# A two-layer transformer in fixed slots on one core: an even slot's gated products before its biases, layer norms on another engine, experts spread over every third slot

## The reference

```python
xn = _layernorm(x)
x = x + L0_attn(xn) + L0_ffn(xn)
xn = _layernorm(x)
x = x + L1_attn(xn) + L1_ffn(xn)
```

## Time and profile before

| | |
|---|---|
| runs | 2309.81, 2303.06, 2306.30 us; median 2306.3 us |
| profiled execution | 2310.34 us, its span 2308.5 us |
| PE busy | 2078.7 us, 90% |
| DVE busy | 1635.0 us, 71% |
| ACT busy | 1400.3 us, 61% |
| POOL busy | 1147.4 us, 50% |
| mean granted clock of PE | 0.971 |

### The profile page before, as it was taken

The page is one execution under the profiler, slowest core; times in us unless marked ns, Lnnn a source line. Parts: engine busy times, 40 slices in busy tenths (PEclk is TensorE's granted clock), DMA queues, the critical chain, the costliest instruction groups (busy, mean ns, idle before and its releaser), DMA issues.

```text
span 2308.5 us, 52509 instructions
## 1 busy us (share of the span) xinstructions
PE 2078.7 (90%) x18761; PEld 1355.0 (59%) x18761; DVE 1635.0 (71%) x5384; ACT 1400.3 (61%) x3797; POOL 1147.4 (50%) x1800
## 2 busy tenths in 40 slices
PE   3888989989899998989989899998989999898988
PEld 1455655656566574655656566574655656566565
DVE  7557767677777767767677776767767677766756
ACT  1667566665756657566665756657566575756642
POOL 5675463745536454463645636454463745535220
PEclk7779999999999999999999999999999999999999
DMA  4000000000000000000000000000000000000000
GB/s 119 6 6 2 1 15 1 15 2 11 6 2 15 1 15 2 1 15 2 15 2 7 10 2 15 2 15 2 1 15 2 15 2 11 1 2 11 2 10 6
DMA packets 33542, 22.03 MB, mean 10 GB/s; under 512 B 2443, under 2 KB 32771, under 8 KB 33283
## 3 DMA queue, kind: packets, MB, share of 16 engines
q1 hardware_dynamic: 33283, 18.68, 2.8%
HBM read 14.48 MB, written 4.19 MB: 8 GB/s over the span
## 4 chain that ended last, share of the span: by engine, by line
PE 60%; DVE 16%; ACT 13%; issue 8%; POOL 4%; DVEq 0%; ACTq 0%; POOLq 0%
PE ps L1097 9%; PE ps L1168 9%; PE ps L1178 7%; PE ps L1237 7%; PE ps L1111 6%; ACT ring L921 4%; PE ps L1087 3%; PE ps L1066 3%; DVE ring L538 3%; ACT pb L930 3%; PE ps L1075 2%; PE ps L1222 2%; PE ps L1144 2%; PE ps L1195 2%; PE ps L1207 2%
## 5 line engine op out<-in xcount | busy, mean ns | idle before, releaser
L814 POOL TENSOR_SCALAR ring<-ring,row_rcp,tau_row 128x128 f32<-128x128 f32 (+3 forms) x1024 | 626.1, 618 | 824.4 <-DVE row_rcp L545 824.2
L921 ACT ACTIVATE ring<-ring,neg_max 128x128 f32<-128x128 f32 (+3 forms) x1024 | 572.2, 560 | 625.6 <-DVE neg_max L538 622.3
L1097 PE MATMUL ps<-identf,ring 128*128 128x128 f32 x2560 | 384.9, 288 | 17.9 <-ACT qkT L912 11.3
L930 ACT ACTIVATE pb<-ps 128x512 f32<-128x512 f32 x640 | 349.1, 585 | 23.9 <-PE ps L1097 16.8
L538 DVE CUSTOM_DVE_ANT_1 ring<-ps,bias_t 128x384 f32<-128x384 f32 (+1 forms) x496 | 287.2, 615 | 82.3 <-PE ps L1087 78.3
L1097 PEld LDWEIGHTS ps<-identf,ring 128*128 128x128 f32 x2560 | 280.1, 144 | 103.8 <-issue 62.6
L1168 PE MATMUL ps<-xn1T,eg_t 128*128 128x512 f32 (+1 forms) x480 | 265.1, 635 | 37.2 <-DVE h L592 36.9
L1237 PEld LDWEIGHTS ps<-ed_t,h 128*128 128x128 f32 (+1 forms) x1920 | 250.7, 191 | 74.7 <-issue 73.1
L1237 PE MATMUL ps<-ed_t,h 128*128 128x128 f32 (+1 forms) x1920 | 272.3, 278 | 0.0
L1178 PE MATMUL ps<-xn1T,eu_t 128*128 128x512 f32 (+1 forms) x480 | 259.3, 622 | 0.4 <-DVE h L599 0.4
L944 ACT ACTIVATE tanh_t<-ps 128x512 f32<-128x512 f32 (+2 forms) x304 | 171.9, 565 | 123.0 <-PE ps L1168 118.3
(11 more groups left out here) (161 smaller groups left out, 3208.2 us busy)
## 6 DMA issues: line engine op xcount, KB each, us to landing
x_t<-x SPq DMA_DIRECT2D x16, 256.0 KB, 2.8
x<-x SPq DMA_DIRECT2D x16, 256.0 KB, 2.8
out<-x SPq DMA_DIRECT2D x16, 256.0 KB, 2.3
bias_t<-bias SPq DMA_DIRECT2D x1, 1536.0 KB, 7.7
eg_t<-eg SPq DMA_DIRECT2D x1, 860.0 KB
eu_t<-eu SPq DMA_DIRECT2D x1, 860.0 KB
ed_t<-ed SPq DMA_DIRECT2D x2, 320.0 KB
ring<-inv_row SPq DMA_DIRECT2D x1, 256.0 KB, 2.7
```

The costliest lines, as they stand in the source:

```text
L814: pool.tensor_scalar(e, e, row_rcp[:, m % 2, r:r + 1], tau_row[:, i, HG * g + r:HG * g + r + 1], ALU.mult, ALU.add).then_inc(p_ok.sem, 1)
L921: act.activation(e, e, ACT.Exp, bias=neg_max[:, n % 2, r:r + 1], scale=-1.0, accum_out=row_sum[:, n % 2, r:r + 1]).then_inc(exp_ok.sem, 1)
L930: act.activation(pb[:, c % NPB, :], bank(turn_bank(q)), ACT.Relu).then_inc(t_taken[q % 2].sem, 1)
L1097: last = pe.transpose(o[:, r * P:(r + 1) * P], ring_of(i, r)[:, k * P:(k + 1) * P], idf)
```

## The change

1. On DVE the gated products (`products`) of an even slot are issued ahead of its two biases. In odd slots they stay where they were.
2. `norm` moves from DVE to ACT: four `activation(Identity)` with the scale `rstd` and a bias `shift = -mean * rstd`, which DVE computes in one small instruction (`norm_shift`). Adding the residual (`ADD_X1`) comes one slot earlier, and with it the statistics and the norm of layer 1 (slot 16). Behind the layer-0 norm the FP4 steps of `x` come one slot later on DVE and POOL.
3. Expert units stand three slots apart, `L1 + 26 + 3 * u`: slots 26 to 62 and, for the last two units of the shared expert, slots 1 and 4 of the next frame. Down products have places of their own; those of the shared expert are at slots 14, 17, 20 and 24 of the next frame, and the result is stored after that. The last frame gets 26 slots instead of 8.
4. `x1` has two buffers, by the parity of the batch, since a batch's residual now lives while the next one's is begun. The output bank's tickets (`plan.y`) are counted in the order of the plan.
5. `pv` of a head group's first row tile stands four slots behind its transposes, the others two as before.
6. The hidden FP4 steps (`HID_STEP`) come at 34 instead of 36, and two pieces of layer 0's constant future term 4 slots later.

```diff
-HID_AMAX, HID_STEP, HID_SCALED = [p + 3 for p in GATE0], 36, (38, 39, 40, 41)
+HID_AMAX, HID_STEP, HID_SCALED = [p + 3 for p in GATE0], 34, (38, 39, 40, 41)
...
-WO, WO_LAST, ADD_X1 = (L1 + 7, L1 + 8, L1 + 9, L1 + 11), L1 + 12, L1 + 14
+WO, WO_LAST, ADD_X1 = (L1 + 7, L1 + 8, L1 + 9, L1 + 11), L1 + 12, L1 + 13
...
-GATE1 = [L1 + 25 + 5 * u // 2 for u in range(3 * NE)]
-DOWN1 = [GATE1[3 * e + 2] + 4 for e in range(NE - 1)] + [L1 + 65]
+GATE1 = [L1 + 26 + 3 * u for u in range(3 * NE)]
+DOWN1 = [tuple(L1 + p for p in places) for places in ((36, 37, 39, 40), (48, 49, 50, 51), (55, 57, 59, 60), (63, 65, 65, 66), (78, 81, 84, 88))]
...
     def blocks_before(self, f, s):
 
-        return self.blocks(*divmod(SLOTS * f + s - 2, SLOTS))
+        near, far = (self.blocks(*divmod(SLOTS * f + s - back, SLOTS)) for back in (2, 4))
+        return [blk for blk in far if STEPS[blk[1]][1] == 0] + [blk for blk in near if STEPS[blk[1]][1]]
...
-        x1 = sb("x1", [P, T, D])
+        x1 = sb("x1", [P, 2, T, D])
...
-            def norm(b, layer, src, dst):
+            def norm_shift(b, layer):
                 dve.wait_ge(rstd_ok[layer].sem, rstd_ok[layer].at(b, 1))
-                for t in range(T):
-                    dve.tensor_scalar(dst[:, t, :], src[:, t, :], moments[:, layer, t, 0:1], rstd[:, layer, t:t + 1],
-                                      ALU.subtract, ALU.mult).then_inc(xn_ok[layer].sem, 1)
+                dve.scalar_tensor_tensor(out=shift[:, layer, :], in0=moments[:, layer, :, 0], scalar=-1.0, in1=rstd[:, layer, :],
+                                         op0=ALU.mult, op1=ALU.mult).then_inc(shift_ok[layer].sem, 1)
...
+                if s % 2 == 0:
+                    for b, p in plan.beside(f, s):
+                        products(b, p)
                 if has(f) and s % 2 == 0:
                     biased(f, s)
                     biased(f, s + 1)
                 for b, p in plan.beside(f, s):
                     for name, k in at(EXTRAS, p):
                         from_scores(b, name, k)
-                for b, p in plan.beside(f, s):
-                    products(b, p)
+                if s % 2:
+                    for b, p in plan.beside(f, s):
+                        products(b, p)
...
+            def norm(b, layer, src, dst):
+                act.wait_ge(shift_ok[layer].sem, shift_ok[layer].at(b, 1))
+                for t in range(T):
+                    act.activation(dst[:, t, :], src[:, t, :], ACT.Identity, bias=shift[:, layer, t:t + 1],
+                                   scale=rstd[:, layer, t:t + 1]).then_inc(xn_ok[layer].sem, 1)
```

More of the change, by code:

```diff
@@ L131, in __init__ @@
                         gate_ticket(("up", layer, b, places.index(p - 1)), 1)
+                if p == WO_LAST:
+                    self.y["first", b] = len(self.y)
+                for e in range(NE):
+                    if p == DOWN1[e][T - 1]:
+                        self.y[e, b] = len(self.y)
         self.unit = {key: n for n, key in enumerate(self.units)}
@@ L138, in slots @@
         for f in range(-1, self.nb + 2):
-            for s in range(SLOTS if f <= self.nb else 8):
+            for s in range(SLOTS if f <= self.nb else TAIL):
                 yield f, s
@@ L206, in build @@
         rstd = sb("rstd", [P, 2, T])
+        shift = sb("shift", [P, 2, T])
         xn = sb("xn", [P, T, D])
@@ L289, in build @@
         rstd_ok = two("rstd_ready")
+        shift_ok = two("norm_shift_ready")
         xn_ok = two("xn_ready", T)
@@ L701, in urgent @@
                 if p == 2:
-                    norm(b, 0, x_t, xn)
+                    norm_shift(b, 0)
                 if 0 <= p - QKV0 - 1 < T:
@@ L705, in urgent @@
                 if p == ADD_X1:
-                    dve.wait_ge(y_ps.sem, y_ps.at(b, 1))
-                    dve.wait_ge(x1_in.sem, x1_in.at(b, 16))
-                    dve.tensor_tensor(x1[:, :, :], x1[:, :, :], bank(Y).rearrange("p (t d) -> p t d", t=T),
+                    dve.wait_ge(y_ps.sem, plan.y["first", b] + 1)
+                    dve.wait_ge(x1_in[b % 2].sem, x1_in[b % 2].at(b // 2, 16))
+                    dve.tensor_tensor(x1[:, b % 2, :, :], x1[:, b % 2, :, :], bank(Y).rearrange("p (t d) -> p t d", t=T),
                                       ALU.add).then_inc(y_taken.sem, 1)
                 if p == ADD_X1 + 1:
-                    dve.wait_ge(y_taken.sem, y_taken.at(b, 1))
-                    norm_stats(b, 1, x1)
+                    dve.wait_ge(y_taken.sem, plan.y["first", b] + 1)
+                    norm_stats(b, 1, x1[:, b % 2, :, :])
                 if p == ADD_X1 + 3:
-                    if has(b + 2):
-                        dve.wait_ge(t_ps.sem, plan.turn["xq", b + 2, 0] + 1)
-                    norm(b, 1, x1, xn1)
+                    norm_shift(b, 1)
                 if 0 <= p - QKV1 - 1 < T:
@@ L934, in store_o @@
                 if g == 0 and b:
[L935 removed]
+                    act.wait_ge(y_ps.sem, plan.y["first", b - 1] + 1)
                 act.copy(o_stack[:, g, :], bank(PV)).then_inc(os_ok.sem, 1)
@@ L948, in elu_exp @@
                 act.activation(elu_m[:, t % 2, :], elu_m[:, t % 2, :], ACT.Exp).then_inc(elue_ok.sem, 1)
-            def beside(b, p):
+            def norm(b, layer, src, dst):
[3 more added lines that the diff above has]
+                                   scale=rstd[:, layer, t:t + 1]).then_inc(xn_ok[layer].sem, 1)
+            def beside(b, p):
+                if p == 2:
+                    norm(b, 0, x_t, xn)
+                if p == ADD_X1 + 3:
+                    if has(b + 2):
+                        act.wait_ge(t_ps.sem, plan.turn["xq", b + 2, 0] + 1)
+                    norm(b, 1, x1[:, b % 2, :, :], xn1)
                 if p == TURN_X:
@@ L1189, in down0 @@
             def down0(b, t):
-                if t == 0 and b:
-                    pe.wait_ge(y_taken.sem, y_taken.at(b, 0))
+                if t == 0 and plan.y["first", b]:
+                    pe.wait_ge(y_taken.sem, plan.y["first", b])
                 wait_turned(("hid", b, t))
@@ L1279, in beside @@
                 for e in range(NE):
-                    if 0 <= p - DOWN1[e] < T:
-                        down1(b, e, p - DOWN1[e])
+                    for t in range(T):
+                        if p == DOWN1[e][t]:
+                            down1(b, e, t)
             for f, s in plan.slots():
```

51 lines of the change are left out of this document (26 added, 25 removed).

## The result

The changed kernel takes 2381.2 us (median of 4 runs, 2380.4 to 2382.4) against 2305.0: a ratio of 1.033, interval 1.031 to 1.035. I had forecast 2236 us, with a range of 2188 to 2288. It is 76 us slower than the kernel before.

What follows compares the result with a forecast made beforehand. PE bounds the kernel, busy 90% of the span, so its 229.8 us idle and its clock can change. Idle -66, clock -5, ends +1 give -70: profiled 2310.3 to 2240, forecast 2236 us, range 2188 to 2288.

Steps and rivals of the forecast that it cites:

- The sum by stretches: Middle frame: PE's idle time falls by 4.4 us, from 11.0 to 6.6; fifteen frames: 66 us.
- the clock's term: Frames 1 to 14: shorter pauses take a third off the 15 us lost to clock falls, 5 us.
- Slots 44-51: The other gate wait, 1.1 us, goes since silu is a slot early; idle 1.9 to 0.7 us, gain 1.2.
- Slots 12-19: Hidden first, norm off DVE and two down products, against a later tanh: idle 3.2 to 1.4 us, gain 1.8.
- Slots 52-63: PE's idle time in this stretch stays at 0.4 us, gain 0.
- slots 0-11: More PE work from late units and the layer-0 norm off DVE: 0.4 us idle left, gain 0.5.
- 32-43: An up and a down product now stand before the scores that waited behind lin: 0.7 us left, gain 0.9.
- Even slots wait for `tanh`: Rival: with odd-slot expert gates, silu ahead of biases makes biases, exps and relu copies hang on tanh; 2341 us, chance 0.07.
- three signs of being wrong: PE waits for biases in even slots behind silu; slots 20-31 give back none or all idle time; busy PE time changes.
- Slots 20 to 31: Gate and pv waits, 2 us, go but return as score waits for biases; idle stays 3.0, bounds 1.0 to 4.5.
- The clock's rival: Slots 25 to 28 so empty for PE that two clock falls come in each frame: +31 us, 2272, chance 0.07.
- The norm on ACT: Slots 12-19: four norm instructions take 1.6 us on ACT; tanh is that late, 0.65 left beyond a down product.

Runs made afterwards that it cites:

- e1: Changed kernel with the gated products behind the biases again in even slots: 2329.3 us, 1.011 of the kernel before.
- e2: Changed kernel with the four instructions of each norm back on DVE in the same slots: 2362.1 us, 1.024 of the kernel before.
- e5: Called the rest: the change without its DVE order, norms on ACT, experts' places and pv move: 2276.2 us, 0.987 of the kernel before.
- e6: e5 plus only the order on DVE, gated products ahead of the biases in even slots: 2334.3 us, 1.013 of the kernel before.
- e7: e5 plus only the new places of expert units and down products: 2296.9 us, 0.997 of the kernel before.
- e8: e5 plus only the norms on ACT: 2279.7 us, 0.989 of the kernel before.
- e9: e5 plus gated products ahead of the biases in even slots for layer 0 alone: 2287.7 us, 0.992 of the kernel before.
- e13: e5 with the residual's addition, statistics and norm of layer 1 back at slots 14 to 17: 2303.8 us, 0.999 of the kernel before.
- e4: Changed kernel with pv of the first row tile two slots behind its transposes again: 2382.2 us, 1.034 of the kernel before.
- e12: e7 with DVE's copy of the layer-0 stack ahead of the gated products in its slot: 2277.8 us, 0.987 of the kernel before.
- e16: Changed kernel with biases first, ACT's late exp as in e11, and the stack copy ahead of DVE's products: 2277.3 us, 0.986 of the kernel before.
- e11: e5 with the late exp: ACT's exp of slot s+1 behind the copies and tanh of slot s: 2237.8 us, 0.970 of the kernel before.

## Why the prediction was wrong

**The sum by stretches was too low in every stretch.** The step that failed is this sum, with the clock's term behind it: I had 6.6 us idle in a middle frame and 5 us less busy time, and frame 7 has 13.9 us idle and PE 37.6 us more busy time. PE's idle time in frame 7 by slots, in us, length less busy time as before:

| | 0-11 | 12-19 | 20-31 | 32-43 | 44-51 | 52-63 | all |
|---|---|---|---|---|---|---|---|
| before | 0.9 | 3.2 | 3.0 | 1.6 | 1.9 | 0.4 | 11.0 |
| expected | 0.4 | 1.4 | 3.0 | 0.7 | 0.7 | 0.4 | 6.6 |
| changed | 1.7 | 2.3 | 3.8 | 2.0 | 2.3 | 2.0 | 13.9 |
| changed, biases first (e1) | 1.1 | 1.6 | 3.3 | 2.1 | 1.6 | 1.2 | 10.9 |
| changed, norms on DVE (e2) | 1.7 | 0.7 | 3.8 | 1.6 | 1.9 | 1.6 | 11.3 |
| the rest (e5) | 1.1 | 1.5 | 3.0 | 1.5 | 1.9 | 0.1 | 9.1 |
| rest + order (e6) | 0.9 | 1.8 | 3.5 | 1.5 | 2.0 | 1.1 | 10.8 |
| rest + experts' places (e7) | 1.1 | 0.8 | 3.9 | 2.1 | 2.0 | 0.9 | 10.8 |
| rest + norms on ACT (e8) | 0.9 | 3.0 | 3.0 | 1.6 | 1.9 | 0.1 | 10.4 |

*Slots 44-51.* I let the gate's wait go because DVE had room on average (busy 14.9 of 18.6 us). What I didn't follow was the second queue: in slot 46 the order makes the bias late, ACT's exps late with it, and behind them the copies. The expected 0.7 us left there is 2.3. The order has 0.7 of these 1.6 us (e1). The rest of the miss comes without it: with the experts' places alone the gate's wait is gone and the stretch is as idle as ever (e7, 2.0), since waits for the copies `nd` (0.8) and `qkT` (1.0) stand there instead.

*Slots 12-19.* I gave the order and the norms 1.8 us a frame. The order costs there (0.3 us on the rest, 0.7 in the changed kernel; e9: 11 us in all), and the norms on ACT cost 1.5 to 1.6 us (e8 against e5, changed against e2), not the 0.65 of my sum. A gain of 1.8 us is real, but it belongs to the addition one slot earlier (e13: 3.3 us idle there, e5: 1.5), which I had listed and given no price.

*The other stretches.* Slots 52-63 were to stay at 0.4 us, without a reason given, and have 2.0: on the rest the order brings 1.0 us there and the places 0.8. The gains that I booked for slots 0-11 (0.5) and 32-43 (0.9) did not come either; with the places alone the latter has 2.1 us.

**A rival named the mechanism and I gave it 0.07.** "Even slots wait for `tanh`": DVE's waits in the changed kernel, against the earlier trace rows:

```profile
DVE h L601 <- ACT tanh_t L955: 115.6, 111, 2.3
DVE ring L547 <- PE ps L1110: 83.1, 71, 2.9
```

The experts' `silu` waits 111 times instead of 36, and the biases wait for PE 83 us instead of 176: their room was used up. With the biases first (e1) it is 61 times and 134 us. The rival's point of decision, the room in front of a bias, looked only at the score banks. They did give way (waits for biases 3.2 us in frame 7, 1.4 in e1), and the banks of the transposes did so beside them (4.9 us, 3.7 in e1). The rival named the exps and copies on that path, but had no price for them. By parts the order costs 52 to 58 us and so turns a gain of 29 into a loss alone. Two of my three signs of being wrong came: waits for biases behind products, and a change in PE's busy time.

**Slots 20 to 31 did not stay.** "I expect these 2 us to return" was right, and they came with more: 3.8 us idle for 3.0. The silu of slot 27 (where a `hidden` stood) holds DVE's copy of the stack until ACT's `tanh`, and PE waits 1.7 us in slot 28. My upper bound of 4.5 held. The places have 0.9 of the idle time by themselves (e7), the order 0.5 (e6).

**The clock's rival was right too.** It falls behind that pause in frame after frame. Around slot 28 of frame 7:

```profile
1062.50:1064.60 2.10, 0.47 (x4) 0.23 (x3) 1.63 (x5) 1.95 (x6) 0.68 (x2) 1.00 0.18 52
1064.60:1068.00 3.40, 3.08 (x9) 2.17 (x10) 2.96 (x11) 2.11 (x5) 2.22 (x5) 0.52 0.16 47
```

In the second window, behind the wait, the granted clock is at its lower level (1.2 GHz) nearly throughout, although PE is busy in it. It falls so at slot 28 or 29 in each of the frames 1 to 15. The Trainium skill says that pauses of PE in a loop bring the clock down again and again (TensorE: Matmul & The Clock Gate, "HAM oscillation — how this bites in real kernels"); the trace agrees that the fall repeats with the loop, behind a pause of 1.7 us that is shorter than those of the page's example. This fall goes with the experts' places: the other kernels that have them fall at slot 29 too (e1 and e2 in all frames 1 to 15, e4 in 13 of them, e12 in 14, e7 in 11, e16 in 4), those with the old places never fall there, and at slot 27 in seven frames or fewer. Frame 7 has two falls, and its busy time is 130.3 us against 126.4; frame 8 before had two and 3.1 more. I had taken 5 us off for fewer falls. PE's busy time grew by 37.6 us instead, 35 of them in the frames 1 to 14 (1784.8 to 1820.1 us). The clock's records put PE at the lower level for 121 us of these frames, and for 45 before; half of the difference, 38 us, is what the lower level costs by estimate, and that is all of the growth there. The rival's price was 31 us.

**The parts do not add.** The rest at 2276 plus 58, 21 and 3.5 gives 2359, and `pv` added nothing; the changed kernel has 2381. The norms cost 3.5 us on the rest, 19 in the changed kernel and 14 with the late exp. In idle time of PE they cost much the same in all three: 21, 24 and 17 us. What differs is busy time, which they lower by 15 us on the rest and by 3 in the other two, for with the norms alone (e8) no fall of the clock begins in the frames 1 to 14. Its frame 7, and most of those frames:

```profile
962.30:1098.80 136.50, 126.12 (x1173) 83.02 (x1173) 97.22 (x330) 90.22 (x246) 71.48 (x113) 1.00 0.03 7
156.00:2054.40 1898.40, 1753.89 (x16281) 1152.54 (x16280) 1353.39 (x4569) 1253.75 (x3404) 990.32 (x1554) 1.00 0.02 7
```

By estimate from the mean clocks (0.982 for 0.977) the clock gives back about 11 us there. So the 3.5 us are not the price of the waits. Why a kernel that idles more keeps its clock is open. `pv` is a smaller case of it: against e4 the changed kernel has 13 us less idle and 15 more busy time.

**What held.** The norm on ACT: 1.6 us for four was the price I took, and it is 26.2/16 = 1.64:

```profile
L964 ACT ACTIVATE xq<-x,shift,rstd 128x128 f32<-128x128 f32 x64 | 26.2, 486 | 8.4 <-DVE shift L506 8.4
...
L964 ACT ACT_TABLE_LOAD x1 | 1.3, 1283 | 8.1 <-DVE shift L506 8.1
```

The wait behind it in slot 18 is 1.6 us, not 0.65: the down product of slot 17 covered nothing that the times show, since the norms cost slots 12 to 19 as much without it (e8, 1.5 us). There is one table load. That the rule of the Trainium skill (ScalarE: Activation LUTs, "Rules for kernel authors"), VectorE for multiply and add, does not fit this tile I concluded from one exp's 0.40 us; the four norms' instructions have 0.49 each and start 0.41 apart, beside 0.47 and 0.62 on DVE. For layer 1 that is 26.2 us on ACT and 26.3 on DVE for the 64 of them, so there neither engine was the faster one. The times say that the move was a loss all the same, 3.5 to 19 us, since what counted was the place in ACT's queue. The `lin` wait of slot 40 is gone, but its time stands in smaller pieces (1.4 us for 1.5), none longer than 0.4. DVE's busy time in the frame fell by 4.4 us and ACT's grew by 2.1, as I had said.

One wait I had not thought of: L1258, 0.7 us in this frame. The shared expert's first down product in slot 14 needs the bank that the residual's addition frees in slot 13. The trace does not name a releaser. The addition ran from 1035.46 us for 0.68, and the product started at 1036.24; that one waits for the other is read from this and from the code, and was not tried.

## What to carry to other kernels

When a wait of the bound engine goes, follow every queue that the move makes later, not only the one it shortens: here DVE's order reached PE through the score banks that the biases empty, and through ACT's exps and the two banks that the copies behind them free. A move that costs no time on its own engine can cost more than it wins on the next one; look for the instruction that stands idle longest (ACT's exps, 622 us in all before) and for what is queued behind it, for that is where a reordering paid here: the second exp behind the copies gave 38 us. A thin stretch for the bound engine can cost twice, once as a wait and again as slower work behind it. And part the time into the bound engine's idle and busy time before a move is called cheap: the norms' 3.5 us were 21 of waits with 15 of busy time given back.

## What the runs showed of the hardware

The granted clock fell at the same place of every middle frame behind a wait of 1.7 us, and not in the frame shown of a kernel that is idle for 7.3 us of it in other pieces (1.00 in the row of e11), nor in any frame from 1 to 14 of one that is idle for 10.4 us in the frame shown (e8). So how long PE idles in a frame did not decide it by itself. In the kernel before, with two waits of 0.74 and 1.32 us in slots 26 and 27, it fell in some frames and not in others.
